# Second layer's attention on one Trainium2 core: the value products move between the second turns and the middle scores, and a reciprocal and an exponential change place

## The reference

```python
q, k, v = einsum('bsx,xMnd->Mbnsd', x, qkv)          # 16 heads of 64
a = einsum('bnsd,bntd->bnst', q, k) * 64 ** -0.5
a = softmax(a + bias, axis=-1)                        # bias: table by distance, -30000 above the diagonal
mix = einsum('bnst,bntd->bnsd', a, v)
return einsum('bnsd,ndx->bsx', mix, out_w)
```

## Time and profile before

| | |
|---|---|
| three runs | 2363.06, 2355.05, 2357.43 us |
| profiled execution, span from first to last instruction | 2391.1 us |
| mean granted TensorE clock | 0.943 |
| TensorE busy / weight loads | 2121.2 us (89%) / 1329.9 us |
| VectorE, ScalarE, GpSimd busy | 1636.0, 1318.1, 941.8 us |
| first call of `attention` | about 150 to 396 us of the span |
| second call | about 563 to 1346 us |

### The profile page before, as it was taken

The page is one execution under the profiler, slowest core; times in us unless marked ns, Lnnn a source line. Parts: engine busy times, 40 slices in busy tenths (PEclk is TensorE's granted clock), DMA queues, the critical chain, the costliest instruction groups (busy, mean ns, idle before and its releaser), DMA issues. The chain is left out here.

```text
span 2391.1 us, 51165 instructions
## 1 busy us (share of the span) xinstructions
PE 2121.2 (89%) x19252; PEld 1329.9 (56%) x19252; DVE 1636.0 (68%) x4801; ACT 1318.1 (55%) x2688; POOL 941.8 (39%) x1175
## 2 busy tenths in 40 slices
PE   4679998998999999999999697799999985899876
PEld 2447776996667776777777565233333333333333
DVE  7665653675555566666666554799899955588896
ACT  2246765555666677777777433167666673323312
POOL 2036665663557743565433122111111110054462
PEclk8689999999999999999999899599999998999998
DMA  6311112214011100000000035211111101000000
GB/s 174 115 52 34 36 33 63 74 37 144 17 35 17 34 6 7 15 2 19 2 2 2 11 97 164 59 36 37 37 39 45 43 7 37 0 0 0 9 9 18
DMA packets 77908, 93.78 MB, mean 39 GB/s; under 512 B 10145, under 2 KB 56242, under 8 KB 76002
## 3 DMA queue, kind: packets, MB, share of 16 engines
q1 hardware_dynamic: 64178, 77.23, 10.8%
q0 software_dynamic: 13488, 13.28, 2.8%
HBM read 54.55 MB, written 35.53 MB: 38 GB/s over the span
## 5 line engine op out<-in xcount | busy, mean ns | idle before, releaser
L1069 ACT ACTIVATE WA<-a_E 128x1024 f32<-128x1024 f32 (+1 forms) x320 | 282.9, 939 | 126.5 <-PE a_E L1002 68.1
L982 PE MATMUL a_S<-a_KS,a_QS 54*128 54x512 bf16 (+3 forms) x768 | 201.8, 352 | 38.2 <-DVE a_mx L1104 27.1
L455 POOL TENSOR_SCALAR WA<-WA,a1b_rinv 128x1024 f32<-128x1024 f32 (+3 forms) x192 | 140.5, 747 | 236.6 <-DVE a1b_rinv L754 236.5
L747 DVE COPY a1b_PT<-a1b_A 128x512 f32<-128x512 f32 x96 | 66.3, 691 | 183.4 <-PE a1b_A L554 183.4
L572 PE MATMUL a1b_O<-a1b_PT,WA 128*64 128x128 f32 x3072 | 190.0, 277 | 0.8 <-DVE WA L747 0.8
L572 PEld LDWEIGHTS a1b_O<-a1b_PT,WA 128*64 128x64 f32 x3072 | 167.0, 137 | 41.2 <-issue 34.3
L535 PE MATMUL a1b_B<-a1b_Kf,a1b_Qf 64*128 64x512 f32 (+2 forms) x768 | 187.2, 484 | 1.3 <-DVE a1b_firstmax L741 1.1
L455 POOL TENSOR_SCALAR XR<-XR,a1b_rinv 128x768 f32<-128x768 f32 (+3 forms) x192 | 140.8, 748 | 115.9 <-DVE a1b_rinv L754 115.9
L982 PEld LDWEIGHTS a_S<-a_KS,a_QS 54*128 54x128 bf16 x768 | 53.5, 94 | 205.1 <-DVE a_mx L1104 97.1
L1020 PE MATMUL a_O<-WA,V 128*9 128x512 f32 (+3 forms) x1536 | 158.0, 499 | 0.1
L1102 DVE TENSOR_REDUCE a_mx<-a_S 128x1 f32<-128x512 f32 x256 | 156.8, 681 | 1.7 <-PE a_S L982 1.7
(11 more groups left out here) (497 smaller groups left out, 5382.5 us busy)
## 6 DMA issues: line engine op xcount, KB each, us to landing
WA<-in_w SPq DMA_DIRECT2D x8, 1024.0 KB, 9.2
a_QS<-qstack SPq DMA_DIRECT2D x32, 216.0 KB
a_KS<-kstack SPq DMA_DIRECT2D x32, 216.0 KB
a1b_tb<-tab SPq DMA_DIRECT2D x12, 512.0 KB
qstack<-f_parts SPq DMA_DIRECT2D x24, 256.0 KB
kstack<-f_parts SPq DMA_DIRECT2D x24, 256.0 KB
f_slots<-f1r_zrows SPq DMA_DIRECT2D x9, 516.0 KB
f1t_xs<-f_slots SPq DMA_DIRECT2D x9, 516.0 KB, 7.1
```

The lines of the kernel that those rows point to most:

```text
L455: pool.tensor_scalar(v, v, rinv[:, e, u, part:part + 1], 1.0, ALU.mult, ALU.mult).then_inc(n_sb, 1)
L982: ins = pe.matmul(pS[(at + half) % SB][:, lo:lo + n], QS[s][ROW[half], pair, i * P:(i + 1) * P], KS[s][ROW[half], pair, c * CH:c * CH + n] ...
L1069: act.activation(PT[q % NP][:, :, 0:w], pE[q % 2][:, :, 0:w], ACT.Exp).then_inc(e_sb, 1)
```

## The change

Three lines move; nothing is added or removed.

1. TensorE: `values(step - 1)` stood at the end of the step, behind the second projection. It now stands behind `turn(step, 1)` and ahead of `scores(step + 2, 1)`.
2. ScalarE: `exponential(step + 1, 0, 1)` now stands ahead of `copy(step, 2)`, where it stood behind it.
3. VectorE: `inverse(step + 1, 0)` now stands ahead of the first bias of the middle piece, where it stood behind the second bias of that piece and behind `copy(step, 2)`.

```diff
@@ TensorE, in the loop over steps
                     turn(step, 1)
+                    if step:
+                        values(step - 1)
                     scores(step + 2, 1)
                     scores(step + 2, 2)
                     turn(step, 2)
@@ TensorE, at the end of the step
                         project(pC[1], it + 2, 0, 0)
-                    if step:
-                        values(step - 1)
             values(ALL - 1)
@@ ScalarE
                     exponential(step + 1, 1, 0)
+                    exponential(step + 1, 0, 1)
                     copy(step, 2)
-                    exponential(step + 1, 0, 1)
                     exponential(step + 1, 1, 1)
@@ VectorE
                         bias(step + 2, order[0], u)
+                    inverse(step + 1, 0)
                     bias(step + 2, order[1], 0)
                     copy(step, 2)
                     bias(step + 2, order[1], 1)
-                    inverse(step + 1, 0)
                     for u in range(HG):
                         bias(step + 2, order[2], u)
```

## The result

The changed kernel takes 2346.60 us (median of four runs, 2345.89 to 2347.72). The kernel before took 2358.89 in its session (four runs, 2355.05 to 2363.06). The ratio is 0.9945, 95% interval 0.9932 to 0.9958: 12.3 us won, where the forecast had 36.6. The time lies inside the range, the sign is right, and the size is off by a factor of three.

A forecast was written before the change was run, and what follows sets the result against it. TensorE (7.64 us a step) and the chain through GpSimd's scalings (7.69) nearly meet, taken as 7.70. Gains of 7.4, 20.4, 6.4 and 2.4 sum to 36.6 us off 2357.4: 2321, range 2302 to 2349.

The forecast's parts named there:

- The step that failed: The 33.7 us between profiled span and timed median lies outside the two attention calls, so 36.6 won carries over unscaled.
- the 20.4 us of the gather stretch: 28 steps of the second call with gathers on GpSimd fall from 8.43 to 7.70 us each.
- does nothing measurable: Rival: chain and tile changes return most of what the waits took, 7.95 us a step, 2348; chance 0.07.
- TensorE's own work: TensorE's step without its wait: 7.50 us plus 0.14 for one more tile-shape change, 7.64.
- surplus "for the weights": Last scores on TensorE: some 0.03 us for weights added to half of 0.91, giving 0.49 for 256 columns.
- The change of tile shape: TensorE's array changes tile shape four times a step instead of three, costing 0.14 us, bounds 0 and 0.27.
- The chain: Middle scores, biases, second reciprocal on VectorE, then GpSimd's scalings up to the next second turns: 7.69 us a step.
- The two exchanges at nothing: Moving the first reciprocal on VectorE and an exponential on ScalarE forward costs nil.
- The cover of 0.4: ScalarE's second exponential ends at 4.8 at worst, middle scores reach VectorE at 5.2, so the early reciprocal delays nothing.
- the normalise chain takes over: Rival: VectorE stands at the first reciprocal with middle scores ready, second scaling slips, 8.3 us a step, 2393; chance 0.10.
- The step with the table change: The 12.41 us step where ScalarE changes its activation table: 2.4 us won from covered waits, bounds 0 and 4.6.
- The last steps: Three steps without projections lose 3.3 us a call, two behind them win some 3: net 0, bounds -6 and +3.

The follow-up runs named there:

- again3: The kernel before, unchanged, profiled again in a later session: 2359.66 us, span 2357.8.
- after_again: The changed kernel, unchanged, run again in another session: 2347.89 us, ratio 0.9764 to the kernel before there.
- again: The kernel before, unchanged, profiled a second time in another session: 2406.31 us, ratio 1.0005 to the kernel before there.
- recip2_early: The changed kernel with the second reciprocal moved between the two last biases on VectorE: 2329.12 us, ratio 0.9695 to the kernel before.
- pe_only: The kernel before with only the value products moved, both exchanges left out: 2455.48 us, ratio 1.0206 to the kernel before.
- swaps_only: The kernel before with only the two exchanges, value products left in place: 2450.89 us, ratio 1.0192 to the kernel before.
- again2: The kernel before, unchanged, in one more session: 2388.93 us in one run, span 2387.1.

## Why the forecast was too large

**The step that failed** is the sentence "I take that distance as lying outside these two calls and carry the difference over unscaled". The 33.7 us lay mostly inside the calls. Against again3, whose span is 33.3 us shorter, the first profile has 27.4 us more in the two calls (244.7 + 760.5 against 237.7 + 740.0). The chain of the argument was right for the execution that it was worked out from; the timed runs, by their time and by the copies of the changed kernel's profile beside them, were executions of another kind, in which no copy was held back. With the steps of again3 the forecast's own terms give 23 x 0.09 = 2.1, 28 x 0.10 = 2.8, 58 x 0.10 = 5.8 (the 6.4 of the text had 7.81) and 2.4 for the table change: 13.1 us. Measured were 12.3 in the medians and 11.9 between the spans 2357.8 and 2345.9. That these agree so well is in part luck. In the stretches that the sum adds up the change won 19.5 (3.2 in the first call, 4.2, and 12.1 in the quiet stretch with its long step), and 7.6 were lost elsewhere: 3.3 in the first and last steps of the calls, and 4.3 outside them. The stretch behind the second call accounts for 3.9 of the 4.3 (1043.6 against 1039.7 in again3); it is 1046.8 in after_again, so it moves by as much with the kernel unchanged, and the 4.3 need not be the change's. The largest term of the sum, the 20.4 us of the gather stretch, was won only where the copies had been late; at the level of the first timed runs it was 4.2 (218.38 to 214.21). In the session of again it was 24.3 of the 57 us that the change is worth there, with 15.1 more in the first call.

That 2346.6 lies at the price of the rival "does nothing measurable" (2348) is a coincidence of numbers: its 7.95 us a step was not seen. (The 8.07 given there as the mean before is 8.05 by the earlier trace rows; nothing hangs on it.)

**TensorE's own work: forecast 7.64, measured about 7.5.** The direct evidence is recip2_early, where the second turns hardly wait: 7.52. Two terms were off.
- The last scores take 0.43 and 0.22, the third turns 0.22; I had 0.49, 0.28 and the 0.29 of the earlier trace rows. No run shows the surplus "for the weights" that I had added: 256 columns take 0.43, and half of 0.91 is 0.46. Some 0.1 a step too much.
- The change of tile shape was sized right. The second turns' section is 0.60 ahead of the value products, where it was 0.49 ahead of scores, and the middle scores take 0.75 after them, where they took 0.71: 0.15 together, forecast 0.14 for one added change. The two projections and the value products keep their 1.91 and 2.11, so nothing is saved where the products stood. The Trainium skill, "TensorEngine Tiling (Array Packing)", Key Properties, says that changing the mode drains the engine. The trace agrees in kind, with this excess of 0.15 us around the products; no run here isolates the drain. Over some 120 steps with value products that is an estimated 18 us which the move gives back.

**The chain: forecast 7.69, measured 7.65.** It was right in its mechanism, and it paces the kernel: recip2_early has the second reciprocal some 0.4 us earlier (6.76 to 7.09 after the first turns) and the step falls by 0.10 to 0.14, to TensorE's own work. It was wrong in its distribution. In quiet steps with e = 0 nothing waits (7.49), in those with e = 2 the second turns wait 0.14 (7.75); the mean is between. The second reciprocal stood at 7.17 to 7.50 after the first turns, where I had 5.85 + 1.47 = 7.3.

**The two exchanges at nothing: right only in company.** The first reciprocal comes 3.9 to 4.2 after the first turns, the middle scores reach VectorE at 5.1 (1023.59 to 1028.72). The cover of 0.4 that I counted at the worst is 0.76 there. But without the moved value products it is negative, and the exchanges cost 46 us; without the exchanges the move costs 50. Both are against the kernel before at 2405. The steps of pe_only have one length with and without transfers, so against the level of 2360 its cost would be some 95 us, an estimate (2455.5 - 2360.2). The rival "the normalise chain takes over" had VectorE stand at the first reciprocal with the middle scores ready. That is the kernel swaps_only (8.12 in quiet steps, 8.79 and 8.96 with transfers). In pe_only the second scaling slips as the rival says, to 8.5 us a step, but because the reciprocal comes late and not early.

**The step with the table change: forecast 2.4 won, measured 4.0.** It takes 8.39. One row says what is left of its two waits (TensorE, third turns):

```profile
898.22 0.34 PE L554 MATMUL a1b_C<-ident,XR 64*128 64x64 f32 x4 [0.38 <-ACT a1b_PT L677]
```

The first wait is covered whole, of the second 0.38 us remain. The waits before were 0.74 and 2.19 (931.72 in the earlier trace rows, and the third turns at 935.32), so 2.55 of them went, near the 2.4 forecast. The other 1.5 are in TensorE's busy time, which fell from 9.49 to 8.02: behind the long wait, from the third turns (935.32) to the end of the step, the granted clock was 0.71 (the lower level, 1.2 GHz, for a part of it), and it is 1.00 in the whole step after. The forecast had no term for that, though the earlier trace rows shows the 0.86.

**The last steps: forecast net 0 a call.** The three steps without projections lost 2.4 (22.15 against 19.78; I had 3.3). The step behind them takes 6.67 and took 8.80 in again3, 2.1 won (I had some 3 for two steps); its granted clock was 0.81 there and is 1.00 now, so this too is not waits alone. Net 0.2 lost in the second call: right.

**GpSimd's transfers, costed at "nil, and up to 0.5 us a step if they run long".** The place was right, the sign was not considered. They start 1.4 us later in the step, at 1.46 to 2.16 after the first turns. There no copy of first turns is late in any of 52 steps, in all three profiles of the changed kernel. The copies of the second turns are late instead where a session holds them (28 of 28 steps with gathers in after_again), but the 2.11 us of value products stand between them and the turns that need them. This is why the kernel's time does not move with the session.

**The gather stretch's waits.** I had named them correctly, and had not asked what delayed a copy of finished turns by 0.7 us. The row names the last semaphore (PE, L554), and by the trace TensorE had long been done.

## What to carry to other kernels

When a profiled span stands 1.4% away from the timed median while other runs have span and time 2 us apart, they are two kinds of execution: find the stretch in which a profile can differ before any term of a sum is taken from it, and give the forecast for both. A wait in which two engines start at the same moment, and the named releaser was long done, belongs to neither: look for what else was issued just before. And an exchange that costs nothing beside a move may cost 2% without it, so of a change with several parts the cover of each is worked out with and without the others.

## What the runs showed of the hardware that was not expected

- The issue of an indirect transfer by GpSimd, started 0.08 to 0.48 us after a group of transposes, delays the engines that wait for them: copies start at 0.91 to 1.52 us instead of 0.75, with no DMA traffic in between in the step looked at. With gathers (L1534) that is 1.3 us after the start of the issue, with the scatters of the first call (L1518) 0.58. It happens in most such steps in some sessions (46 to 48 of 52 in before, again and again2) and in none in another (0 of 52, same starts). One kernel so has levels of 2359, 2393 and 2405 us. In the changed kernel the issue starts 1.4 us later, no copy of first turns is held, and those of second turns that are held (1.30 to 1.41 us in after_again) cost nothing, because the value products cover them.
- The value products between transposes and scores, with the change of the array's tile shape on either side, cost 0.15 us a step beyond the work: 0.10 in the section of transposes that ends at the first value product, 0.05 in the scores that follow the products.
- A wait of 2.19 us of TensorE was followed by a granted clock of 0.71 over the next 5.95 us (935.32 to 941.27); with the wait cut to 0.38 the clock stayed at 1.00, and TensorE's busy time in the step was 1.5 us shorter.
